# A two-layer selective scan: when TensorE's products, ScalarE's table changes and GpSimd's sums stand in the chunk

## The reference

```python
# x: (1, 8192, 512) fp32; two Mamba layers, then a soft mixture of experts
x = x + layernorm(mamba(layernorm(x)))
x = x + layernorm(soft_moe(layernorm(x)))
# one Mamba layer (1024 inner channels, 16 states, 4 taps, rank 32)
xc, z = split(x @ W_in.T)
u = silu(causal_depthwise_conv(xc, w_c) + b_c)
dt, Bm, Cm = split(u @ W_x.T)                      # 32, 16, 16 columns
delta = softplus(dt @ W_dt.T + b_dt)
h[t] = exp(delta[t] * A) * h[t-1] + delta[t] * u[t] * Bm[t]   # for each channel and state
y[t] = sum over 16 states of h[t] * Cm[t]  + u[t] * D
out = (y * silu(z)) @ W_out.T
```

## Time and profile before

| | us |
|---|---|
| median of three runs | 8613.19 |
| profiled execution | 8617.45 |
| span of its trace | 8615.6 |
| ahead of the first scan | 238.9 |
| from the first scan of the first chunk to the end of the last one | 7523 |
| behind it (mixture of experts) | 854 |

### The profile page before, as it was taken

One profiled execution on the slowest core, in us unless ns is written; L12 is line 12 of the kernel. 1 busy time (PEld: TensorE's weight loads), 2 busy tenths in 40 slices (PEclk: granted clock), 3 DMA queues, 4 the chain that ended last, 5 costly groups with the idle time before them and its releaser, 6 DMA issues. The chain is left out here.

```text
span 8615.6 us, 126403 instructions
## 1 busy us (share of the span) xinstructions
PE 7396.0 (86%) x31688; PEld 4113.0 (48%) x31688; DVE 7620.8 (88%) x8802; ACT 5873.9 (68%) x10702; POOL 6574.0 (76%) x2826
## 2 busy tenths in 40 slices
PE   5788888888888888888888888888888888876886
PEld 3444444444444444444444444444444444445753
DVE  2899999999999999999999999999999999995717
ACT  5777777777777777777777767777777777754415
POOL 0888888888888888888888888888888888881103
PEclk7899999999999999999999999999999999977889
DMA  5111111111111111121111111111111111114434
GB/s 197 49 51 50 46 50 51 51 51 52 53 51 47 51 52 49 45 63 61 61 51 52 51 52 46 51 51 48 46 50 51 51 52 50 47 37 153 166 127 148
DMA packets 223573, 552.99 MB, mean 64 GB/s; under 512 B 26272, under 2 KB 26528, under 8 KB 201824
## 3 DMA queue, kind: packets, MB, share of 16 engines
q1 hardware_dynamic: 196448, 459.30, 17.0%
q10 hardware_dynamic: 26368, 84.95, 2.5%
HBM read 442.44 MB, written 101.71 MB: 63 GB/s over the span
## 5 line engine op out<-in xcount | busy, mean ns | idle before, releaser
L931 POOL TENSOR_TENSOR bu<-w,b_rep 128x1024 f32<-128x1024 f32 x2048 | 4808.6, 2361 | 956.0 <-DVE h L1007 955.9
L1007 DVE TENSOR_TENSOR_SCAN h<-decay,h_last,bu 128x512 f32<-128x512 f32 x3840 | 4817.3, 1271 | 200.1 <-PE turn L519 140.6
L728 ACT ACTIVATE decay<-delta,neg_a 128x512 f32<-128x512 f32 x4096 | 2802.7, 689 | 1862.4 <-DVE h L1007 1848.1
L519 PEld LDWEIGHTS turn<-ident_m,h 128*128 128x128 f32 x16384 | 1918.4, 143 | 3163.2 <-DVE acc L1027 1246.1
L519 PE MATMUL turn<-ident_m,h 128*128 128x128 f32 x16384 | 2591.6, 282 | 615.3 <-DVE acc L1027 359.3
L1027 DVE SCALAR_TENSOR_TENSOR acc<-turn,c_now,acc 128x512 f32<-128x512 f32 x3200 | 2327.5, 727 | 191.9 <-PE turn L519 185.8
L448 PE MATMUL proj<-conv_in,conv_diag 128*128 128x512 f32 x2048 | 1039.7, 596 | 45.7 <-ACT halo L662 45.7
L448 PE MATMUL proj<-x_conv,w_in 128*128 128x512 f32 x2048 | 1055.5, 613 | 22.0 <-DMA x_conv<-xt 17.0
L448 PE MATMUL proj<-x_gate,w_in 128*128 128x512 f32 x2048 | 1034.2, 597 | 43.1 <-ACT stage L718 29.5
L448 PE MATMUL proj<-zy,w_out 128*128 128x512 f32 x2048 | 1033.7, 599 | 0.9 <-DVE zy L1036 0.9
L946 POOL TENSOR_TENSOR acc_v<-acc_v,prod 128x1024 f32<-128x1024 f32 x320 | 755.2, 2360 | 16.7 <-ACT prod L742 16.7
(11 more groups left out here) (171 smaller groups left out, 5947.0 us busy)
## 6 DMA issues: line engine op xcount, KB each, us to landing
b_rep<-b_rows SPq DMA_DIRECT2D x1024, 256.0 KB, 3.3
x_conv<-xt SPq DMA_DIRECT2D x32, 1024.0 KB, 6.5
x_gate<-xt SPq DMA_DIRECT2D x32, 1024.0 KB, 4.8
xt<-stage ACTq DMA_DIRECT2D x128, 256.0 KB, 2.4
x_n<-in_x_dram SPq DMA_DIRECT2D x16, 1024.0 KB, 5.2
xt<-xt_n ACTq DMA_DIRECT2D x16, 1024.0 KB, 4.3
x_l<-in_x_dram SPq DMA_DIRECT2D x16, 1024.0 KB, 5.8
mt_l<-xt SPq DMA_DIRECT2D x16, 1024.0 KB, 6.3
```

Source lines behind the costliest of these rows:

```text
L519: mm = pe.transpose(out[:, b * P:(b + 1) * P], h[:, k % 2, b, j * P:(j + 1) * P], ident[:])
L728: act.activation(decay[:, b, :], delta[:, blk, :], ACT.Exp, scale=neg_a[:, n, blk:blk + 1]).then_inc(decay_set, 1)
L931: pool.tensor_tensor(bu[:, s // 2 % 4, :, :], w[:, blk:blk + 2, :], b_rep[:, k % 4, :].unsqueeze(1).to_broadcast([P, 2, T]), ALU.mult).the ...
L1007: dve.tensor_tensor_scan(h[:, k % 2, b, :], decay[:, b, :], bu[:, s // 2 % 4, b % 2, :], start, ALU.mult, ALU.add).then_inc(scanned, 1)
```

## The change

- The order of products and the rule that places them are new: each slot has room for a constant time, less what its turn tiles take (WEIGHT, in products), in place of 1.17 products a slot.
- Skip tiles move from slots 0 to 3 and 32 to 35 to slots 4 to 7 and 30, 33, 36, 39; the second `y` tiles from 20, 22, 24, 26 to 22, 24, 26, 28.
- SiLUs are placed by `silu_at`, clear of ScalarE's turn tiles; before, they stood at ScalarE's slots 0, 37, 61 and 114; after, at 2, 42, 65 and 119.
- ScalarE takes a turn tile at slot s+2, not s+3.
- All 16 pairs of states give a `prod` tile (14 before). `prod` has three buffers, one of which holds the running sum; `acc_v` goes.
- GpSimd's delta sums and products stand four of its steps apart (W_AT), not one.

The diff, cut to its core:

```diff
-RATE = 1.17
-TAKE_LAG, TAPS_LEAD, W_LAG, X_PROJ_LAG, XDBL_LAG, CONV_LAG, PROD_LAG = 4, 2, 10, 5, 3, 4, 3
+TAKE_LAG, TAPS_LEAD, XDBL_LAG, CONV_LAG, PROD_LAG = 4, 2, 4, 4, 2
+W_AT = {17: ("sum", 2), 21: ("product", 2), 25: ("sum", 3), 29: ("product", 3),
+        49: ("sum_next", 0), 53: ("product_next", 0), 57: ("sum_next", 1), 61: ("product_next", 1)}
-Y0_AT = (116, 118, 120, 122)
-Y1_AT = (20, 22, 24, 26)
-SKIP_AT = (0, 8)
+Y_AT = ((116, 118, 120, 122), (22, 24, 26, 28))
+SKIP_AT = ((7, 4, 5, 6), (30, 33, 36, 39))
+WEIGHT = {"x_proj": 1.1, "delta": 1.25, "delta_next": 1.25, "turn_c": 0.5, "state": 0.55, "skip": 1.05, "y": 0.55}
+def silu_at(end):
+    at = end + TAKE_LAG
+    behind = (at - PROD_LAG - 5) % (2 * J)
+    return at if behind < 5 else at + 2 * J - behind
 def timetable():
-    at, end_of = 0.0, {}
+    room = [-sum(WEIGHT[tile[0]] for tile in tiles_at) for tiles_at in TURN_AT]
+    whole = sum(PRODUCTS[kind] * WEIGHT.get(kind, 1.0) for kind, _, _ in ORDER) - sum(room)
+    room = [r + whole / (SLOTS_BODY - 3) for r in room]
...
-        slots = [int(at + q / RATE) for q in range(PRODUCTS[kind])]
-        at += PRODUCTS[kind] / RATE
+        slots = []
+        for q in range(PRODUCTS[kind]):
+            while left < WEIGHT.get(kind, 1.0) / 2 or slot < earliest:
+                slot += 1
+                left = min(left, 1.0) + room[slot]
+            slots.append(slot)
+            left -= WEIGHT.get(kind, 1.0)
...
-V_PAIRS = [q for q in range(GROUPS // 2) if q % HALF_Q != 2]
-V_SET = {q: i % 2 for i, q in enumerate(V_PAIRS)}
+V_BUFFER = (0, 1, 2, 1, 2, 1, 2, 1, 2, 1, 0, 1, 0, 1, 0, 1)
 def by_act(tile):
-    return tile[0] == "skip" or tile[0] == "state" and tile[1] // 2 in V_PAIRS and tile[2] == V_AT[tile[1] % 2]
+    return tile[0] == "skip" or tile[0] == "state" and tile[2] == V_AT[tile[1] % 2]
...
-            more = prod[:, 1 - V_SET[q]] if q % HALF_Q == 1 else acc_v[:]
-            pool.tensor_tensor(acc_v[:], more, prod[:, V_SET[q]], ALU.add).then_inc(vsum_set, 1)
+            total = prod[:, V_BUFFER[q - q % HALF_Q]]
+            pool.tensor_tensor(total, total, prod[:, V_BUFFER[q]], ALU.add).then_inc(vsum_set, 1)
```

More of the change, by code:

```diff
@@ L48 @@
 PAIRS = SLOTS_BODY // 2
-RATE = 1.17
-TAKE_LAG, TAPS_LEAD, W_LAG, X_PROJ_LAG, XDBL_LAG, CONV_LAG, PROD_LAG = 4, 2, 10, 5, 3, 4, 3
+TAKE_LAG, TAPS_LEAD, XDBL_LAG, CONV_LAG, PROD_LAG = 4, 2, 4, 4, 2
+W_AT = {17: ("sum", 2), 21: ("product", 2), 25: ("sum", 3), 29: ("product", 3),
+        49: ("sum_next", 0), 53: ("product_next", 0), 57: ("sum_next", 1), 61: ("product_next", 1)}
 NOT_FIRST = ("out",)
 NOT_LAST = ("conv_half", "conv", "x_proj", "delta_next", "turn_c")
-def timetable():
-    at, end_of = 0.0, {}
[L57 to L66, removed]
-        slots = [int(at + q / RATE) for q in range(PRODUCTS[kind])]
-        at += PRODUCTS[kind] / RATE
-        for slot in sorted(set(slots)):
-            lo = slots.index(slot)
-            work[slot].append((kind, x, i, lo, lo + slots.count(slot)))
-        end = end_of[kind, x] = slots[-1]
-        if kind == "conv_half":
-            take[end + TAKE_LAG - TAPS_LEAD].append(("taps", x, i))
-        take[end + TAKE_LAG].append((kind, x, i))
[L76 to L85, removed]
@@ L107 @@
+LAST_SKIP = [("skip", hf, SKIP_AT[hf].index(max(SKIP_AT[hf]))) for hf in range(2)]
 TURNS = 2
@@ L117, in turn_tiles @@
             carried.append(order[s][-1])
[L118 to L124, removed]
+        for hf in range(2):
+            if s in SKIP_AT[hf]:
+                order[s].append(("skip", hf, SKIP_AT[hf].index(s)))
+            if s in Y_AT[hf]:
+                order[s].append(("y", hf, Y_AT[hf].index(s)))
+                if hf == 1:
+                    carried.append(order[s][-1])
@@ L737, in product @@
                 act.wait_ge(c_set, 2 * G + (k // HALF_C + 1))
[L738 to L742, removed]
+            emptied, in_last = emptied_before(q)
+            if k % 2 == 0 and not (kind.first and in_last):
+                behind = in_last and emptied not in SUMS_CARRIED
+                at = SUMS.index(emptied) - len(SUMS) if behind else kind.sums.index(emptied)
+                act.wait_ge(vsum_set, sum_base(G, kind) + (at + 1 + C_PROD))
+            act.activation(prod[:, V_BUFFER[q], k % 2, :], turn[:, BANK[tile], :], ACT.Copy,
                            scale=c_now[:, j, n:n + 1]).then_inc(v_done, 1)
@@ L969, in body @@
             for p in range(PAIRS):
-                for what, pair in W_AT[p]:
-                    if kind.has(what.replace("sum", "delta").replace("product", "delta")):
-                        delta_w(G, what, pair)
+                what, pair = W_AT.get(p, ("", 0))
+                if what and kind.has(what.replace("sum", "delta").replace("product", "delta")):
+                    delta_w(G, what, pair)
                 k, pr = divmod(p, 2)
```

73 lines of the change are left out of this document (49 added, 24 removed).

## The result

The changed kernel takes 8875.38 us (median of 4 runs, 8873.12 to 8879.51). The kernel before, run beside it, takes 8615.08. The ratio is 1.030 (95% interval 1.0285 to 1.0321). I had said 8480 and faster; it is 260 us slower.

The account below looks back on a forecast made before the run. VectorE was taken as the bound: floor 218.4 plus 12.15 us of waits made 230.6 a first-layer chunk (3.8 less), 231.4 a second-layer one (4.6 less). That took 134 us off 8617.45: 8483, said as 8480; range 8310 to 8610.

Parts of the forecast that it names:

- Adds: On VectorE, 4 of 100 adds a chunk go to ScalarE: 2.6 us a chunk less, 82 us in all.
- GpSimd's 0: GpSimd's two more operations a chunk charged nothing; bounds 0 and 2.3 us at each of four delta steps.
- Takes one slot earlier: ScalarE's takes with lag 2: bounds 0.6 gained per freed bank, 0.7 lost per take; 0 taken.
- SiLUs: ScalarE's moved SiLUs: nothing at slots 2 and 65, waits at 43 and 48, and 1.3 us at slot 120.
- The second's terms: SiLU at slot 42: waits of 1.6 us at slot 43 and 0.75 at slot 48.
- The order of products: Products waiting for banks: 1.3 us each at slots 88 and 96, 0.85 at 24 to 32, 0.2 at 12 and 16.
- Skip tiles: Leaving slots 0 to 3 clears waits there; new waits of 1.1 us at slot 6, 0.8 each at 8 and 40.
- The edge: Where the loop turns, 3.56 us of TensorE issue stays; the scan of slot 0 waits 1.8 us.
- The range: 8310 to 8610 us, from waits of 6.5 (half of A) to 15.5 (most of B).
- C: Rival, chance 0.12: early takes wait 0.7 us in each of 16 pairs, 11.2 a chunk; slower, about 8840.
- A: Rival, chance 0.14: the waits go for good, only the edge and two of 0.8 us remain; about 8200.
- B: Rival, chance 0.12: new waits, 16 us in place of 13.4, eat the adds' gain; about 8600.

Follow-up runs that it names:

- e4: Changed kernel with ScalarE taking turn tiles and skip copies at slot s+3 again (PROD_LAG 3), SiLUs kept in place: 8710.12 us, 1.011.
- e5: Changed kernel with ScalarE's takes at slot s+3 and the first SiLU of z at ScalarE's slot 116: 8611.15 us, 1.000.
- e6: e5 with the next chunk's four delta projections standing singly, in the order of the kernel before: 8559.39 us, 0.993.
- e9: Changed kernel with the order and placing rule of the kernel before, lag 3, SiLU of z at 114, SiLUs of u at 40 and 64: 8549.94 us, 0.992.
- e11: e7 with GpSimd's delta sums and products spread four of its steps apart: 8533.40 us, 0.991.
- e7: Kernel before with all 16 pairs on ScalarE and three prod buffers, nothing else of the change: 8535.31 us, 0.991.
- e1: Changed kernel with the first SiLU of z at ScalarE's slot 116 in place of 119: 8761.65 us, 1.017.
- e3: Changed kernel with the edits of e1 and e2 together: 8633.70 us, 1.003.
- e13: e11 with PROD_LAG 2 in place of 3, nothing else: 8668.82 us, 1.007.
- e2: Changed kernel with the next chunk's four delta projections standing singly, in the order of the kernel before; SiLU of z stays at 119: 8841.24 us, 1.026.
- e14: e11 with SiLUs of u at 42 and 65, TensorE's first product in slot 4 and 1.22 products a slot: 8441.05 us, 0.980.
- e8: Changed kernel with TensorE turning the tiles of slots 75 to 77 three times, 24 more matmuls a chunk: 8829.64 us, 1.025.

## Why the prediction was wrong

The runs form a path from the changed kernel back to before; each step is one difference of medians.

| step undone | us |
|---|---|
| early takes (changed, e4) | 165 |
| SiLU of z at 119 (e4, e5) | 99 |
| paired delta projections (e5, e6) | 52 |
| rest of the order and the rule, SiLUs 1 to 2 slots earlier (e6, e9) | 9 |
| moved skip tiles, y tiles, SiLUs of u (e9, e11) | 17 |
| GpSimd's spreading (e11, e7) | -2 |
| 16 pairs (e7, before) | -80 |
| sum | 260 |

The 9 and the -2 are within the spread of the runs. A different order of steps shares out the first three otherwise, for they overlap. What the lag alone costs, all else equal:

| else | takes at s+2 | at s+3 | us |
|---|---|---|---|
| as changed | 8875 | 8710 (e4) | 165 |
| z at 116 | 8762 (e1) | 8611 (e5) | 150 |
| z at 116, deltas singly | 8634 (e3) | 8559 (e6) | 74 |
| order of before, 16 pairs | 8669 (e13) | 8533 (e11) | 135 |

So the early takes cost in every order tried. The SiLU's move costs 114 with the rest as changed, 99 with lag 3 and 208 with the deltas singly; the pairing costs 34, 52 and, with z at 116, 128.

*Adds: right*, 78 to 80 against 82. GpSimd's 0 is right too: in the changed kernel VectorE waits for no `bu` between 600 and 7400 us. That holds only while its steps stand behind the delta projections that they read. Where the projections moved and the steps did not (e2, e3, e6, e14), VectorE waits for `bu`.

*Takes one slot earlier: the step that failed most.* I had both bounds right (a loss of up to 0.7 per take) and chose 0, because "a wait of 0.7 in front of a decay that is due 5 us later moves nothing in undisturbed slots". In undisturbed slots that is so, they keep 1.83. The step from there to 0 for the whole chunk failed. The take that stands behind the product on ScalarE frees a TensorE bank and has no 5 us (slots 86, 94, 95). Ahead of a SiLU the 5 us are already spent, so the decay itself comes late (slot 42, 1.3), and so does the SiLU that the gate waits for (slot 116, 1.3). The idle time ahead of `prod`, from 2000 to 4200 us, was 3.9 us in 264 before and is now

```profile
L763 ACT ACTIVATE prod<-turn,c_now 128x512 f32<-128x512 f32 x290 | 198.5, 685 | 188.6 <-PE turn L538 186.7
```

It costs 165 us, 5.2 a chunk.

*SiLUs: failed at the third.* I charged 1.3 at slot 120, for a gate tile's bank, and did not ask who waits for the SiLU itself: the gate in slot 116. It is 4.1 at slot 116 and 2.4 at 119. The second's terms, 1.6 and 0.75, measured 1.3 and 0.7; but the 1.3 is gone with lag 3 (e4), so it belongs to the early takes too.

*The order of products: right in place, too small.* 1.3 and 1.3 at slots 88 and 96 are 3.2 and 5.1 (86 and 87; 94 and 95). I priced everything there at full clock and with ScalarE on time. The early takes added 0.9 of TensorE's 1.33; behind that stand the next four product records took 2.85 us, not 1.88. At slot 95, from 2346.6 to 2352.4 us, the granted clock was 0.51. With lag 3 these places cost 3.5 less in all.

*Skip tiles: right on both sides* in the new order: 0 left at slots 0 to 3, waits of 1.4 and 0.8 at slots 6 and 7. In the old order the same places bring nothing: e9 has waits of 3.4 and 1.7 there and is 17 us slower than e11.

*The edge*: 1.8 charged, 1.0 measured at slot 127. I kept 3.56 us of issue; it is 2.1 to 2.4 in inner chunks of the changed kernel. Its size goes with the place of the last products: 2.9 to 3.6 us where they end in slot 124 (before, e9, e11, e14), 1.9 to 2.8 where they end in 126 (changed, e5, e8). No run moves them alone. A stall of 2 us is left, and with it the trace still agrees with the Trainium skill, "Runtime: NRT & Kernel Launch", Instruction fetch mechanics, and not with the 108 ns of the Trainium skill, "Advanced Engine Details and Errata", Control Flow Timing. But I took the branch for its only place, and in the second layer slots 1 and 2 wait 1.9 and 1.7 us behind a second stretch of issue.

*The range.* By the sum's own steps, waits of 6.5 and 15.5 a chunk give about 8300 and 8585, not 8310 and 8610. The measured time is far outside either.

*The rivals.* C had the mechanism and, at a chance of 0.12, nearly the time, 8840. That it came so near is luck. It charged 16 pairs at 0.7, 11.2 us a chunk; the takes cost 5.2, at a few spots where a bank or a SiLU is next, and the rest of the excess is the SiLU's of `z` and the delta pairs'. Its sign, "products on ScalarE delay turn tiles in every stretch of eight slots", is not what is seen. A and B were out.

## What to carry to other kernels

When a consumer asks earlier for the same work, list what stands behind it in its own queue and whose buffer each of these frees; the shortest slack among them counts, not that of the engine's main stream. When an operation moves, ask first who reads its result, then whom it holds up. When one engine's work moves, look at the steps of the others that read it: here GpSimd's stayed and cost waits in four runs. Try the parts of a change singly: here one part gained 80 us and the others cost some 340 and hid it.

## What the hardware showed beyond that

A wait of TensorE can be followed by a stretch at the lower clock: behind the stand of 3.09 us, with 0.24 us of work in 3.3, came 7.0 us at a granted 0.51, while the 11.3 us from 2332.7 on, without a long stand, kept 1.00. In the changed kernel chunks run at 0.96 and 0.94 against 0.99 and 0.98 before; with lag 3 alone (e4) they run at 0.99 and 0.97. What of the cost is the clock's and what the waits' no run separates.

The issue idle of 2.43 us in the middle of straight code, just behind the loop's branch, was gone when the code ahead had another length (e8). e5 and e9 have it too, at 2.3 to 2.8 and 1.7 to 3.0 us, in the second layer alone. What it is stays open: no run separates the fetching of instructions from another cause, and a shift of the code by a few instructions with nothing else changed was not tried. In the kernel before, the same place is not clear: the tile there needs a bank that VectorE frees only then.
